# Two-layer graph network in hand-ordered code: GpSimd's and VectorE's order in the last iteration

## The reference

```python
h = relu(layernorm(x))
z_l, z_g, v = h @ W_lang.T, h @ W_grav.T, h @ W_V.T
A_l = relu(cosine(z_l, z_l)) * not_eye
A_g = exp(-dist2(z_g, z_g) / (2 sigma^2)) * not_eye
K   = w_l * rownorm(A_l * adj) + (1 - w_l) * rownorm(A_g * adj)
x   = x + (K @ v) @ W_O.T
h2  = relu(layernorm(x))
x   = x + h2 contracted with adj * adj over the nodes + bias
```

## Time and profile before

| | |
|---|---|
| median of 3 runs | 1218.77 us (1218.64 to 1219.27) |
| the profiled execution, its own time | 1218.51 us |
| its span | 1216.8 us |
| TensorE matmul busy | 1197.1 us (98%) |
| VectorE busy | 1055.2 us (87%) |
| ScalarE busy | 714.9 us (59%) |
| GpSimd busy | 603.7 us (50%) |

### The profile page before, as it was taken

The page is one execution under the profiler, slowest core; times in us unless marked ns, Lnnn a source line. Parts: engine busy times, 40 slices in busy tenths (PEclk is TensorE's granted clock), DMA queues, the critical chain, the costliest instruction groups (busy, mean ns, idle before and its releaser), DMA issues.

```text
span 1216.8 us, 22852 instructions
## 1 busy us (share of the span) xinstructions
PE 1197.1 (98%) x6092; PEld 1024.1 (84%) x6092; DVE 1055.2 (87%) x1888; ACT 714.9 (59%) x1326; POOL 603.7 (50%) x988
## 2 busy tenths in 40 slices
PE   7999999999999999999999999999999999999997
PEld 6887888888888888888888888888888888888885
DVE  6668988889888888988888988888988888898878
ACT  5356555566556566556556655556655656655644
POOL 2103665454565454565544465545456545456443
PEclk9999999999999999999999999999999999999999
DMA  7122433434433444433343443344443344443212
GB/s 270 52 85 72 125 111 104 135 129 130 147 109 96 123 135 127 143 112 104 113 141 127 137 122 111 105 136 128 131 147 109 95 124 134 127 144 112 69 45 104
DMA packets 115457, 145.10 MB, mean 119 GB/s; under 512 B 20848, under 2 KB 52720, under 8 KB 115440
## 3 DMA queue, kind: packets, MB, share of 16 engines
q1 hardware_dynamic: 114864, 144.57, 38.4%
q10 hardware_dynamic: 576, 0.33, 0.1%
HBM read 62.46 MB, written 49.87 MB: 92 GB/s over the span
## 4 chain that ended last, share of the span: by engine, by line
PE 95%; DVE 2%; POOL 1%; ACT 1%; issue 0%; DMA 0%; DVEq 0%; ACTq 0%
PE ring L971 50%; PE ring L1068 28%; PE p_ps L1040 15%; PE kt_ps L984 1%; PE ring L1091 1%; DVE x_ring L730 1%; POOL x_ring L346 0%; POOL h_lo L361 0%; DMA x_ring<-in_L_gnn_W_lang 0%; DVE h_lo L715 0%; ACT h L438 0%; DVE bn L883 0%; PE ring L1100 0%; DVE x_ring L690 0%; DVE hT_lo L619 0%
## 5 line engine op out<-in xcount | busy, mean ns | idle before, releaser
L361 POOL TENSOR_TENSOR h_lo<-h2f,h_hi 128x512 fp32r<-128x512 f32 x124 | 156.9, 1296 | 327.4 <-ACT h_hi L538 327.4
L971 PE MATMUL ring<-hT_hi,Lw_hi 128*128 128x512 f32 x640 | 249.4, 390 | 4.2 <-DVE hT_lo L639 1.5
L971 PE MATMUL ring<-hT_lo,Lw_hi 128*128 128x512 f32 x640 | 249.0, 389 | 0.0
L971 PE MATMUL ring<-hT_hi,Lw_lo 128*128 128x512 f32 x640 | 249.0, 389 | 0.0
L619 DVE TENSOR_TENSOR y_lo<-ring,y_hi 128x512 fp32r<-128x512 f32 x256 | 169.3, 682 | 44.8 <-ACT y_hi L459 44.5
L1068 PE MATMUL ring<-MT_hi,hT_hi 128*128 128x512 f32 x512 | 199.3, 389 | 0.0
L1068 PE MATMUL ring<-MT_hi,hT_lo 128*128 128x512 f32 x512 | 199.2, 389 | 0.0
L1068 PE MATMUL ring<-MT_lo,hT_hi 128*128 128x512 f32 x512 | 199.2, 389 | 0.0
L459 ACT ACTIVATE y_hi<-ring 128x512 fp32r<-128x512 f32 x256 | 152.3, 597 | 74.9 <-PE ring L971 71.5
L502 ACT ACTIVATE v_hi<-ring 128x512 fp32r<-128x512 f32 x128 | 76.0, 594 | 184.8 <-PE ring L1068 184.8
L346 POOL TENSOR_TENSOR x_ring<-x_ring,bias_sb 128x512 f32 (+1 forms) x120 | 152.3, 1303 | 0.0
(11 more groups left out here) (184 smaller groups left out, 2536.3 us busy)
## 6 DMA issues: line engine op xcount, KB each, us to landing
x_ring<-in_x SPq DMA_DIRECT2D x32, 1024.0 KB, 5.3
out<-x_ring SPq DMA_DIRECT2D x128, 256.0 KB, 2.6
h_turned<-h SPq DMA_DIRECT2D x496, 64.0 KB, 2.0
p_dram<-chain SPq DMA_DIRECT2D x62, 256.0 KB, 2.3
h<-p_dram SPq DMA_DIRECT2D x248, 64.0 KB, 2.5
rn_cols<-rn_dram SPq DMA_DIRECT2D x31, 256.0 KB, 3.7
x_ring<-in_L_gnn_W_lang SPq DMA_DIRECT2D x4, 256.0 KB, 5.3
h2f<-in_L_gnn_W_grav SPq DMA_DIRECT2D x1, 1024.0 KB, 8.8
```

The source lines that it names most:

```text
L361: pool.tensor_tensor(h2[1][:, b], h2f[:, b], h2[0][:, b].bitcast(F32), ALU.subtract)\
L971: mm = pe.matmul(out, lhsT, rhs, start=(k == 0), stop=(k == len(terms) - 1))
```

## The change

GpSimd in the last pass: `add_bias` of group 29 goes from ahead of `row_norms` to behind `norm2` of group 30. GpSimd behind the pass: `h2_lo` of group 30 for graphs 0, 1 and 2 goes ahead of `last_factors(0)`, and graph 3 ahead of `last_factors(1)`. VectorE: all four `stats` of group 30 stand ahead of `sum_s_last`.

```diff
@@ GpSimd, iteration(i)
                 if lag:
                     for b in range(GB):
                         h2_lo(i - 2, b)
-                    for b in range(GB):
-                        add_bias(i - 2, b)
+                    if after:
+                        for b in range(GB):
+                            add_bias(i - 2, b)
                 if before and after:
                     norm2(i - 1)
                 row_norms(i)
@@ GpSimd, behind the passes
-            last_factors(0)
             h2_lo(g - 1, 0)
             h2_lo(g - 1, 1)
+            h2_lo(g - 1, 2)
+            last_factors(0)
+            h2_lo(g - 1, 3)
             last_factors(1)
-            h2_lo(g - 1, 2)
-            h2_lo(g - 1, 3)
@@ VectorE, last_chain
-                stats(i - 1, 0)
+                for b in range(GB):
+                    stats(i - 1, b)
                 sum_s_last(i)
...
                 v_lo(2)
-                stats(i - 1, 1)
                 kt_lo(i)
                 v_lo(3)
-                stats(i - 1, 2)
-                stats(i - 1, 3)
```

## The result

The changed kernel took 1222.51 us (median of 8 runs, 1221.80 to 1223.18) against 1218.77 us (8 runs, 1217.78 to 1219.27): ratio 1.0033, 95% interval 1.0024 to 1.0042. It is slower by 3.7 us, 0.33%; 1224.0 was forecast, in a range of 1220.5 to 1226.2. Its profiled execution has a span of 1220.9 us, 4.1 more.

A forecast was written before the change was run, and what follows sets the result against it. TensorE bounds up to about 1180 us; then PE and VectorE reach K together, VectorE without a gap. 1.58 + 2.0 + 1.2 + 0.48 = +5.3 us on 1218.5 gave 1223.8, as a median 1224.0 us; range 1220.5 to 1226.2.

The forecast's parts named there:

- hold-up: VectorE's way to K: instructions with two SBUF inputs wait for GpSimd's large additions to end; +2.0 us, bounds 0 and 3.4.
- Row norms ahead of the bias: GpSimd, last pass: PE's 0.52 us wait ahead of L1016 goes; worth up to -0.52 us, booked 0.
- Four statistics ahead of the sum: VectorE's way to K: three more statistics take 1.80 us, PE's transposes of K come later; +1.58 us.
- Two signs named ahead: Signs for the profile after: L828 at about 1184.4, and the transposes of K at 1194 to 1195.
- The bias behind `norm2`: GpSimd's four additions fall beside VectorE's row factors and combine of K, holding up L668, L675 and L680; +2.0 us.
- The clock: TensorE idles longer around the transposes of K, so K v likely starts at 1.2 GHz; +1.2 us, bounds 0 and 2.7.
- The tail: GpSimd's order behind the pass: ACT's h2_full of group 31 waits for last_factors(0), +1.16 us; with two gains, +0.48 us.
- the two gains that I had named: Behind the pass: ACT's first copy of group 30 gains 0.15 us, VectorE's lag behind ACT's last copy goes, -0.53 us.
- The bounds: The forecast's own range, 1221.9 to 1226.2 us, from hold-up 1 to 3 and clock 0.8 to 2.7; chance 0.64.
- only the statistics count: Rival: no hold-up and no low clock, +1.58 + 0.48 = +2.1, 1220.8 us; chance 0.13.
- That K had room: Rival: statistics fit into a hidden wait of VectorE ahead of the sum; 1218.8 us, no change; chance 0.06.

The follow-up runs named there:

- e1: Kernel before with all four statistics of group 30 ahead of the sum, GpSimd's order as before; 1220.51 us against 1218.39, ratio 1.0016.
- e2: Kernel before with the additions of the bias behind the row norms and behind a wait for K of group 31; 1217.91 us against 1218.39.
- e3: Changed kernel with GpSimd's additions of the bias waiting also for K of group 31; 1218.36 us against 1218.39 before, ratio 1.0002.
- e4: Changed kernel with 12 more matmuls on PE ahead of the transposes of K, result overwritten; 1221.71 us, ratio to before 1.0025.
- e6: Changed kernel with GpSimd's old order behind the pass; 1221.85 us, ratio to before 1.0030.
- e5: Kernel before with the additions of the bias behind the row norms, without a wait for K; 1218.61 us against 1218.32, ratio 1.0003.
- e10: Kernel before with two statistics ahead of the sum, additions of graphs 0 and 1 behind the rest of the bias, 2 and 3 behind K; 1216.93 us.
- e9: Changed kernel with each addition of the bias of group 29 in two halves of 128x256; 1223.39 us, ratio to before 1.0042.
- e8: Changed kernel with the additions of the bias waiting for K and GpSimd's old order behind the pass; 1217.93 us against 1218.33 before.

## Why the prediction came out

The sign and the size were right, 1224.0 against 1222.5, but one term was wrong, and it hides in the sum. That the total came so near is partly luck: statistics and hold-up together were booked at 3.58 us, and the transposes of K came 2.04 later, 1.54 too much booked; the clock was booked 0.86 too low, and the two errors stand against each other.

- *Row norms ahead of the bias*, booked at 0. PE's wait ahead of L1016 did go, and K was late, so it was worth nothing by itself.
- *Four statistics ahead of the sum*, booked at +1.58. **This is the step that failed.** The term's own size is right: e1 shows 1.57. But in the changed kernel the sum stands 8.48 us behind the copy of P instead of 8.43. I read L835's 1.81 us as evidence for the hold-up and didn't ask what becomes of that very wait once the additions leave: VectorE's way from its first diagonal to its first residual shrank from 4.59 us (1174.87 to 1179.46) to 2.84 (1174.48 to 1177.32), 1.75 us. e2 shows it alone: K 1.34 us earlier. The removed work's cost on another engine was left out of the part that it was removed from, and the statistics filled it. Two signs named ahead missed for this reason: L828 started at 1182.23 and not at about 1184.4, and the transposes of K at 1192.42 and not at 1194 to 1195.
- *The bias behind `norm2`*, booked at +2.0, measured 2.23, and e3 gives back those 2.23 us. The places were partly others: not `combine`, since the three held-up row factors kept VectorE back until the last addition had ended (1191.09, `combine` at 1191.23), but L673, a `tensor_scalar` with one input, which I had taken as free.
- *The clock*, booked at +1.2, measured 0.47 + 1.59 = 2.06, and e4's profile gives back 2.06. The low level also covered the transposes of K (1.11 us against 0.60), which the term didn't have. How early the clock falls differs between executions: in e6's it fell only behind the transposes.
- *The tail*, booked at +0.48, measured +0.37. Of it the new order costs 0.9 (e6), against the two gains that I had named.
- *The bounds.* The forecast's own range was added up wrongly: with hold-up 1 and clock 0.8 the terms give 1222.6, not 1221.9, and with 3 and 2.7 they give 1226.5, not 1226.2. The measured 1222.5 lies at the lower of these bounds; the range as stated, from 1220.5, holds it because of the cases added to it.

The rivals: that only the statistics count is out by e3. That K had room was half right: no wait of VectorE ahead of the sum was hidden in the old order, but the hold-up of the diagonal was as good as one, 1.75 us that the change itself freed. It didn't win, since the additions took 2.23 us on the other side.

So of the change, taken apart: the place of the additions and the statistics together cost K 2.27 us; the clock makes 2.06 more of it; the order of the tail costs 0.9, of which 0.5 is made up. These sizes are of the profiled executions. Neither of the two parts that were run by themselves, the statistics (e1) and the additions behind the row norms (e5), gave anything to the end (the order of the tail was only taken out of the changed kernel, not put into the one before), and the additions in a better place than either, with a second statistics ahead (e10), do.

## What to carry to other kernels

When GpSimd works in SBUF beside VectorE, moving its instruction is two changes: take VectorE's hold-up out where it stood, and put it in where it goes, and look at both stretches of VectorE's timeline for rows that are longer than their like. Put it beside VectorE instructions that read PSUM or only one tile (here the sum, the statistics and L657 of e5; the `tensor_scalar` named below was an exception), and cut the group there, not each instruction. A delay in front of TensorE can cost double when its clock falls in the gap: here 2.27 us at K and 2.06 for the clock.

## What was unexpected in the hardware

- A VectorE `tensor_scalar` with one SBUF input of 128x8 took 1.22 us instead of 0.17 beside GpSimd's additions, and ended 0.03 us behind one of them. In "SBUF — State Buffer", section "Who interferes with whom", the Trainium skill names `tensor_scalar` as one of those that can enter a two-port mode and then contend; the row agrees. The reciprocal behind it, with one input as well, took its usual 0.20 us at 1188.68, inside the third addition (1188.58 to 1189.86), so that one input is not in itself what decides. A `tensor_scalar` was held up in two other places: L845, 0.42 us before and 0.17 after, and L679 of e9, 0.66 us.
- The hold-up goes the other way as well. GpSimd's power instruction of `norm2`, 1.04 us where VectorE had no instruction with two SBUF inputs running at its start, takes 1.50 us in the changed kernel, where it starts at 1184.36 inside VectorE's first mask with two SBUF inputs (1184.26 to 1184.95).
- The clock of TensorE fell in e3's profile with 0.84 us of idle time ahead of the transposes of K and 1.42 behind them, and stayed up in e8's with the same pattern. It stayed up in e5's too, with 1.31 us ahead of the transposes, and fell in e1's with 1.41. The same program's runs lay in two groups 2 us apart. What decides between them stays open.
